# A state-space block with a gated feed-forward layer: the skip term as scaled transposes at unit 7

## The reference

```
xz = x @ W_xproj.T                       # 96 columns: 64 of rank, 16 of B, 16 of C
dt = softplus(xz[:, :64] @ W_dt.T + b_dt)
h_s = exp(-exp(A_log_s) * dt) * h_s + dt * B_s * x     # over time, for each state s
out = sum_s(h_s * C_s) + Dp * x
x1 = layernorm(x + out)
```

## Time and profile before

| | |
|---|---|
| median of 3 runs | 2003.35 us (2001.41 to 2003.37) |
| the profiled execution | 1997.66 us, of which the span from the first to the last instruction is 1995.8 us |
| PE busy | 1763.8 us, 88% of the span |
| DVE busy | 1823.0 us, 91% |
| ACT busy | 1568.9 us, 79% |
| POOL busy | 1701.3 us, 85% |
| mean granted TensorE clock | 0.95 of full |

### The profile page before, as it was taken

One profiled execution on the slowest core, in us unless ns is written; L12 is line 12 of the kernel. 1 busy time (PEld: TensorE's weight loads), 2 busy tenths in 40 slices (PEclk: granted clock), 3 DMA queues, 4 the chain that ended last, 5 costly groups with the idle time before them and its releaser, 6 DMA issues.

```text
span 1995.8 us, 37091 instructions
## 1 busy us (share of the span) xinstructions
PE 1763.8 (88%) x11048; PEld 1384.4 (69%) x11048; DVE 1823.0 (91%) x2285; ACT 1568.9 (79%) x2924; POOL 1701.3 (85%) x779
## 2 busy tenths in 40 slices
PE   5788888988989988889888989889889898899986
PEld 4667677776777776777666777667767667776764
DVE  4899999999999999999999999999999999999994
ACT  6878878788887788778788787888777887887862
POOL 5998888898888988888888888988889888889880
PEclk7999999999999999999999999999999999999999
DMA  7323333333233233234233233232333332342300
GB/s 243 101 97 120 105 114 117 102 110 117 90 122 124 93 116 116 91 118 133 80 121 117 96 117 126 87 122 97 116 118 98 114 116 87 118 133 70 122 12 22
DMA packets 116565, 215.35 MB, mean 108 GB/s; under 512 B 11153, under 2 KB 45554, under 8 KB 116466
## 3 DMA queue, kind: packets, MB, share of 16 engines
q1 hardware_dynamic: 116466, 214.40, 32.8%
HBM read 195.48 MB, written 18.87 MB: 107 GB/s over the span
## 4 chain that ended last, share of the span: by engine, by line
PE 56%; issue 17%; DVE 16%; ACT 6%; POOL 3%; DVEq 1%; ACTq 0%; DMA 0%; POOLq 0%; SPq 0%
PE p_o L1001 17%; PE p_y L964 12%; DVE h L703 8%; PE p_m L988 6%; PE p_da L932 6%; PE p_c L941 3%; PE p_m L904 3%; DVE hid L747 3%; PE p_m L912 3%; PE p_y L957 2%; PE p_m L978 2%; DVE silu_g L741 2%; ACT da_k L537 2%; ACT p_da L537 1%; POOL ub L410 1%
## 5 line engine op out<-in xcount | busy, mean ns | idle before, releaser
L420 POOL TENSOR_TENSOR h<-h,c_bc 128x1024 f32<-128x1024 f32 x352 | 833.0, 2371 | 148.0 <-ACT h_carry L523 120.7
L410 POOL TENSOR_TENSOR ub<-u,b_bc 128x1024 f32<-128x1024 f32 x320 | 757.7, 2374 | 0.1
L964 PE MATMUL p_y<-ident,h 128*128 128x128 f32 x4096 | 533.3, 277 | 7.7 <-POOL h L420 4.4
L537 ACT ACTIVATE p_da<-dt,neg_a 128x512 f32<-128x512 f32 x640 | 432.1, 682 | 85.3 <-DVE h L703 81.8
L964 PEld LDWEIGHTS p_y<-ident,h 128*128 128x128 f32 x4096 | 476.2, 143 | 28.1 <-POOL h L420 13.6
L703 DVE TENSOR_TENSOR_SCAN h<-p_da,ub 128x512 f32<-128x512 f32 x320 | 381.1, 1213 | 29.8 <-ACT p_da L537 23.6
L703 DVE TENSOR_TENSOR_SCAN h<-p_da,h_carry,ub 128x512 f32<-128x512 f32 x320 | 399.9, 1271 | 1.4 <-ACT p_da L537 0.8
L551 ACT ACTIVATE ub_t<-u_t,bc_t 128x256 f32<-128x256 f32 x768 | 344.9, 497 | 28.9 <-issue 28.1
L1001 PE MATMUL p_o<-wt_down,hid 128*128 128x256 f32 x1536 | 354.8, 382 | 11.8 <-DVE hid L747 8.6
L932 PE MATMUL p_da<-ident,ub_t 128*128 128x128 f32 x1536 | 244.1, 296 | 126.5 <-DVE h L703 125.5
L1001 PEld LDWEIGHTS p_o<-wt_down,hid 128*128 128x128 f32 x1536 | 284.9, 190 | 67.3 <-issue 29.6
(11 more groups left out here) (101 smaller groups left out, 1813.4 us busy)
## 6 DMA issues: line engine op xcount, KB each, us to landing
c_bc<-bc_rows_dram SPq DMA_DIRECT2D x352, 256.0 KB, 5.1
b_bc<-bc_rows_dram SPq DMA_DIRECT2D x128, 512.0 KB, 5.3
x_in<-in_L_attn_x SPq DMA_DIRECT2D x32, 512.0 KB, 3.5
b_bc<-bc_rows_dram SPq DMA_DIRECT2D x64, 256.0 KB, 3.1
out_x<-res_n SPq DMA_DIRECT2D x32, 512.0 KB, 3.3
bc_rows_dram<-bc_rows SPq DMA_DIRECT2D x32, 64.0 KB, 1.6
hid<-in_L_ffn_w_gate SPq DMA_DIRECT2D x1, 768.0 KB, 4.9
hid<-in_L_ffn_w_up SPq DMA_DIRECT2D x1, 768.0 KB, 6.7
```

The lines of the kernel that those rows point to most:

```text
L410: nc.gpsimd.tensor_tensor(ub[:, i % UB_SLOTS, :, :], u[:, par, :, :], b_bc[:, i:i + 1, :].broadcast_to([P, DH, T]), ALU.mult).then_inc(s_u ...
L420: nc.gpsimd.tensor_tensor(h[:, s % H_SLOTS, :, :], h[:, s % H_SLOTS, :, :], c_bc[:, i:i + 1, :].broadcast_to([P, DH, T]), ALU.mult).then_i ...
L537: nc.scalar.activation(da, dt[:, par, q, :], ACT.Exp, scale=neg_a[:, q, s:s + 1]).then_inc(s_da, 1)
L964: ins = nc.tensor.matmul(p_y_tok[:, k, q * P:(q + 1) * P], h[:, s % H_SLOTS, q, k * P:(k + 1) * P], ident[:, :], start=False, stop=(s == S ...
```

## The change

The product with the diagonal goes. ScalarE writes x_skip = (1 + Dp) * x_t for the whole chunk, in two activations of 128x512, one for each half: x_scaled0 in unit 5 (second half) and x_scaled1 in unit 6 (first half). TensorE adds x_skip to p_y by transposes, in two jobs of four transposes of 128x128 (skip0 and skip1, tokens 0 to 255 and 256 to 511), in unit 7, zones 0 and 1, each behind a wait on both activations. p_y is now opened by the transposes of the first state. The prologue's two activations that wrote the diagonal go too.

```diff
+    "skip0": (7, 0), "skip1": (7, 1), "x_scaled0": (5, 1), "x_scaled1": (6, 0),
...
-        skip_diag = sb("skip_diag", [P, DH, P], F32)
+        x_skip = sb("x_skip", [P, DH, T], F32)
...
+            def x_scaled(c, par, q):
+                wait(act, s_y, N * c)
+                nc.scalar.mul(x_skip[:, q, :], x_t[:, par, q, :], skip1[:, q:q + 1]).then_inc(s_x_skip, 1)
...
-            act.wait_ge(s_const, 1)
-            for q in range(DH):
-                nc.scalar.mul(skip_diag[:, q, :], ident[:, :], skip1[:, q:q + 1]).then_inc(s_skip_diag, 1)
...
                         if nxt and due("bc_cols"):
                             bc_cols(c + 1, 1 - par)
+                        for q in range(DH):
+                            if core and due(f"x_scaled{q}"):
+                                x_scaled(c, par, q)
...
             def sum_states(c, s, par):
                 if s == SUM_ORDER[0]:
                     wait(pe, s_z, c)
-                    for k in range(TT):
-                        for q in range(DH):
-                            nc.tensor.matmul(p_y_tok[:, k, q * P:(q + 1) * P],
-                                             x_t[:, par, q, k * P:(k + 1) * P], skip_diag[:, q, :],
-                                             start=(k % 2 == 0 and q == 0), stop=False,
-                                             skip_group_check=True)
                 wait_hc(pe, c, s)
                 for k in range(TT):
                     for q in range(DH):
                         ins = nc.tensor.matmul(p_y_tok[:, k, q * P:(q + 1) * P],
                                                h[:, s % H_SLOTS, q, k * P:(k + 1) * P], ident[:, :],
-                                               start=False, stop=(s == SUM_ORDER[-1]),
+                                               start=(s == SUM_ORDER[0] and k % 2 == 0 and q == 0),
+                                               stop=(s == SUM_ORDER[-1]),
                                                is_transpose=True, skip_group_check=True)
                 ins.then_inc(s_y, 1)
+
+            def skip(c, a):
+                pe.wait_ge(s_x_skip, DH * (c + 1))
+                for k in range(2 * a, 2 * a + 2):
+                    for q in range(DH):
+                        nc.tensor.matmul(p_y_tok[:, k, q * P:(q + 1) * P],
+                                         x_skip[:, q, k * P:(k + 1) * P], ident[:, :],
+                                         start=False, stop=False, is_transpose=True, skip_group_check=True)
...
-            pe.wait_ge(s_skip_diag, 2)
...
+                        for a in range(2):
+                            if core and due(f"skip{a}"):
+                                skip(c, a)
```

More of the change, by code:

```diff
@@ L78, in mamba_ffn_block @@
     assert NB % UB_SLOTS == N % H_SLOTS == NK % K_SLOTS == 0
+    assert all(sum(AT[f"skip{a}"]) > max(SUM_LAG.values()) for a in range(2))
     sum_at = {s: s + SUM_LAG[s in POOL_STATES] for s in range(N)}
@@ L182, in mamba_ffn_block @@
         s_skip1 = sem("s_skip1")
-        s_skip_diag = sem("s_skip_diag")
+        s_x_skip = sem("s_x_skip")
         s_xt_ps = sem("s_xt_ps")
```

## The result

The changed kernel takes 2015.31 us (median; 2014.79 to 2015.62) beside 2002.38 us (1998.99 to 2003.37) of the kernel before in the same comparison: a ratio of 1.0069, 95% interval 1.0054 to 1.0083. That is 12.9 us by the medians. Forecast were 17.6 us more (2021 from 2003.35).

What follows compares the result with a forecast made beforehand. The bound was a ring of unbroken TensorE, ScalarE and VectorE stretches. Mean x1_low shifts of 0.71 us (even) and 0.46 (odd), 0.58 a chunk, over 30 chunks gave 17.5 us on 2003.35: 2021 us, range 2001 to 2036.

Steps and rivals of the forecast that it cites:

- The ring: Unbroken stretches of TensorE, ScalarE and VectorE, each handing over to the next, about 60 us for a chunk.
- The product goes from unit 3: TensorE drops 16 products, 1.79 us; scan (5,0) starts that much earlier, but only 0.17 to 0.2 us remains at state 6.
- The pair: Two scaling activations inside ScalarE's stretch, 0.61 us each, delay decay (8,1) by 1.22; x1_low shifts 0.71 in even chunks.
- Odd chunks: x1_low, after decay (8,1) moved by 1.22 us, comes at 18.20 after softplus_abs against a mean of 17.74: 0.46 later.
- TensorE at unit 7: Eight added transposes, 0.87 us or 1.7 at half clock, cost nothing, with 0.5 us of cover; bounds 0 and 0.3.
- The slowest rival: TensorE's clock stays low, x1_transposed is late and slow, all 1.22 us lands each chunk: 37 us, 2040 us; chance 0.15.
- the prologue against chunk 0: Before the main chunks: 0.6 us saved once by two dropped activations, set against chunk 0's moved ScalarE work.

Runs made afterwards that it cites:

- The product alone out of unit 3: Changed kernel with the product with the diagonal kept, as two jobs of 8 products in unit 7, and no scaling activations on ScalarE: 2000.12 us, ratio 0.9998.
- the pair alone: Kernel before with the two scaling activations added on ScalarE in units 5 and 6, result unused, skip product left in unit 3: 2032.44 us, ratio 1.0160.
- skip spread over the stretch: Changed kernel, scaling activations at unit 4, skip jobs in unit 7 zone 2, one waiting for state 6's first decay, one for its first scan: 1997.90 us.
- the run with skip and a sum held back: Changed kernel, scaling activations at unit 4, skip jobs ahead of state 4's sum also waiting for state 6's first scan: 1984.80 us, ratio 0.9923.

## Why the prediction was right

**The bound.** The ring was read rightly. The product alone out of unit 3 brought 0.8 us, within its interval, where TensorE had 1.79 us a chunk less in a stretch without a break; the pair alone cost 31.5 us where ScalarE's share of the span is 79%.

**The product goes from unit 3.** By its steps: scan (5,0) 2.28 us after softplus_abs (forecast 2.27), dt_of at 5.68 (5.70), scan (6,0) at 7.86 (7.69). Decay (6,0) ends at 1018.35 and the scan starts at 1018.56, 0.2 us later and not 0.04; so it was before too (1008.91 and 1009.12), and even the 0.17 us of gain at state 6 was not there.

**The pair.** 1.22 us forecast, 0.61 each; measured 0.61 to 0.62 each, and decay (8,1) 1.19 us later in even chunks. There x1_low stands at 18.25, forecast 18.21, and the period is 0.72 us longer on average (60.57, chunk 16: 1010.70 to 1071.27, from a mean of 59.86), forecast 0.71.

**Odd chunks: the term that was mis-sized.** Forecast 0.46 us. Measured from ScalarE's and VectorE's timelines of chunk 17, whose softplus_abs is at 1071.27, against the earlier trace rows:

```profile
1086.17 0.71 ACT L539 ACTIVATE da_k<-dt,neg_a 128x512 f32<-128x512 f32 x1
```

```profile
1089.32 1.22 DVE L741 SCALAR_TENSOR_TENSOR x_t<-p_m,x_t 128x1024 f16<-128x1024 f32 x1
```

Decay (8,1) starts at 14.90 instead of 13.90: 1.00 us later, not 1.22. The prediction's term took the whole pair for cost, but in odd chunks ScalarE had a wait within its stretch that the pair filled. Decay (7,0) may not start before scan (6,0) has ended. Before, that scan ended at 1069.74 and the decay followed at 1069.77, 0.99 us after the two activations ahead of it had begun; after, it followed them at 0.80:

```profile
1068.78 0.89 ACT L551 ACTIVATE ub_t<-u_t,bc_t 128x256 f32<-128x256 f32 x2
1069.77 0.69 ACT L537 ACTIVATE p_da<-dt,neg_a 128x512 f32<-128x512 f32 x1
```

```profile
1068.49 1.25 DVE L703 TENSOR_TENSOR_SCAN h<-p_da,h_carry,ub 128x512 f32<-128x512 f32 x1
```

```profile
1080.61 0.89 ACT L557 ACTIVATE ub_t<-u_t,bc_t 128x256 f32<-128x256 f32 x2
1081.41 0.67 ACT L539 ACTIVATE p_da<-dt,neg_a 128x512 f32<-128x512 f32 x1
```

x1_low is at 18.05, forecast 18.20, 0.33 behind the mean of before (17.72). The odd chunk as a whole became only 0.19 us longer. Of the 0.14 between, 0.11 stand between x1_low and the last `hidden`, and most of that in two chunks of the kernel before, 23 and 27. There the low clock lasted until 19.1 us after softplus_abs, through the jobs ahead of the gate products, and VectorE waited 0.35 and 0.31 us for ScalarE's tanh; the two took 0.65 us longer than the rest. Chunk 23, TensorE and VectorE:

```profile
1435.20 0.66 PE L932 MATMUL p_da<-ident,ub_t 128*128 128x128 f32 x4 [3.77 <-DVE h L703]
1436.37 1.11 PE L932 MATMUL p_da<-ident,ub_t 128*128 128x128 f32 x4 [0.52 <-DVE h L703]
```

```profile
1445.34 0.69 DVE L741 SCALAR_TENSOR_TENSOR silu_g<-tanh_g,p_m 128x512 f32<-128x512 f32 x1 [0.35 <-ACT tanh_g L572]
```

The periods of 14 even chunks at 0.72 us and 15 odd ones at 0.19 make 12.8 of the ring's 12.9 us, where 17.5 were forecast.

**TensorE at unit 7.** No cost, as forecast, at half pace (1.97 us). The clock at x1_transposed was forecast not to matter for x1_low, and it doesn't in the changed kernel: VectorE never waits for x1_high there, where the kernel before had such waits in 24 of 30 chunks. But it mattered more for the size than the prediction says: that the decays decide, and not x1_high, is itself the clock's doing. Without it the pair costs 31.5 us. The slowest rival, at 2040 us, was the case in which the clock stays low, and the pair alone shows it at 2032.

The Trainium skill (TensorE: Matmul & The Clock Gate, "Loop structure matters more than you think") says that long waits between matmuls send the clock down and that work without them keeps it up. By that rule the prediction let x1_transposed get faster, and it did, from 54.1 to 32.7 us; but no long wait had gone: TensorE's idle is longer than before (4.46 us in chunk 16) and skip behind it runs at the low clock. What changed is that TensorE resumes 5.7 us ahead of x1_transposed in chunk 16 (1020.36 and 1026.02), where it was 3.1 (1012.77 and 1015.90). As a rule to build by, that of the Trainium skill is too short: with the waits split up and none of them over 1.8 us (skip spread over the stretch) the measured clock fell as before, and the measurement decides. So the prediction's own reading, that the long idle before ub_transposed is what drops the clock, is too narrow.

**Ahead of the ring** the profiled execution is 2.5 us later, where I had set the prologue against chunk 0. The start of the first scan was 25.7 to 26.1 us in seven of the eleven profiled executions and 27.6 to 27.9 in four, with the prologue's pair and without it, so most of this belongs to the one execution. The 0.6 us that the prologue was to give back can't be told in it.

## What to carry to other kernels

Find the ring: follow one engine's unbroken stretch to the next one's start until it closes. Work taken off a busy engine behind the point where it hands over brings nothing, and two small instructions on an engine at 79% cost 0.4 to 1 us a turn if they stand inside its unbroken stretch, nothing where it waits for the hand-over (2032, 2015 and 2002 us for the same pair).

In this kernel work that nobody waits for was best held back into TensorE's idle stretch, in one dense piece ahead of work that is on the path: the clock is then back when it counts (1985 and 1983 us). The length of the piece counted: eight transposes brought 5 us, sixteen, or sixteen products, 16 to 18.

## What the runs showed of the hardware

- Eight transposes (0.9 us) in the middle of TensorE's idle stretch ran at full pace in 18 of 30 chunks and did not keep the clock up; neither did two times four, with no idle over 1.8 us. Behind 3.93 us of idle in chunk 16 the eight transposes of skip ran at 0.213 us each, at 1.2 GHz; TensorE went on, and x1_transposed, which began 5.1 us after them, ran at full pace.
- The clock does not always fall within the idle. In ten of 30 chunks of the kernel before, the first four transposes behind 3.65 to 3.77 us of idle ran at full pace (in chunk 23 above the granted clock was 1.00 in 1435.20 to 1435.80), and the fall came only with what followed (0.50 in 1436.40 to 1440.00).
- In the changed kernel, with TensorE busy without a break on transposes alone, the low clock ended 2.8 us after TensorE resumed in chunk 16 (granted clock 1.00 from 1023.30) and 6.1 us after it in chunks 21 and 22 (0.50 in 1324.40 to 1330.40, then 1.00). In the kernel before x1_transposed starts 3.1 to 3.2 us after TensorE resumes, and takes 1.5 us or more in 24 of 30 chunks.
- The kernel before spreads over 1996 to 2005 us, the changed one over 2014.8 to 2015.6. That a kernel spreads because its path holds such a stretch is not shown: the run with skip and a sum held back has x1_transposed at full pace throughout, and spreads over 1982 to 1989.
- With the clock at full pace the skip products were 0.112 us apart and the transposes 0.109; one fp32 product of 128x128 counts as two instructions (16 for 8 blocks), a transpose as one. Moving the product to a transpose halved TensorE's time for it, here at no gain.
